# Second weights of the expert layers: high and low halves side by side, two products for three, and a sum of two parts on VectorE

## The reference

```
x = x + 0.5 * _L0_ffn_ref(_layernorm(x), Wg, W1, W2)       # moe0
x = x + _L0_attn_ref(_layernorm(x), ...)
x = x + 0.5 * _L0_ffn_ref(_layernorm(x), Wg, W1, W2)       # moe2
x = x + 0.5 * _L1_ffn_ref(_layernorm(x), Wr, W1, b1, W2, b2)   # moe3
x = x + _L1_attn_ref(_layernorm(x), ...)
x = x + 0.5 * _L1_ffn_ref(_layernorm(x), Wr, W1, b1, W2, b2)   # moe6
```

```
h = gelu(x @ w1 + bb1)
y = h @ w2 + bb2
acc = acc + ce[..., None] * y
```

## Time and profile before

| what | value |
|---|---|
| median of 3 runs | 1114.45 us (1113.37 to 1115.78) |
| profiled execution | 1116.47 us, its span 1114.7 us |
| PE busy | 674.6 us, 5992 matmuls |
| DVE busy | 723.4 us |
| ACT busy | 524.2 us |
| POOL busy | 540.8 us |
| adds and copies of `finish` | from 106.0 to 156.9 (moe0), 388.2 to 439.2 (moe2), 547.5 to 668.8 (moe3), 904.2 to 1062.1 (moe6) |

### The profile page before, as it was taken

One profiled execution on the slowest core, in us unless ns is written; L12 is line 12 of the kernel. 1 busy time (PEld: TensorE's weight loads), 2 busy tenths in 40 slices (PEclk: granted clock), 3 DMA queues, 4 the chain that ended last, 5 costly groups with the idle time before them and its releaser, 6 DMA issues.

```text
span 1114.7 us, 20298 instructions
## 1 busy us (share of the span) xinstructions
PE 674.6 (61%) x5992; PEld 531.0 (48%) x5992; DVE 723.4 (65%) x2283; ACT 524.2 (47%) x1160; POOL 540.8 (49%) x562
## 2 busy tenths in 40 slices
PE   7115853589810586343899981488872569977900
PEld 7013531277710354343688870255552458766700
DVE  7884675989988355677355663599988636533542
ACT  3611333756550133251577871377762258755700
POOL 0007656586100562642676766465112656574475
PEclk9998985789955599555799995699885679988965
DMA  9602321000020133121233331111000123222242
GB/s 300 171 0 48 91 60 48 19 4 2 2 76 0 42 83 70 47 81 28 59 85 77 82 62 50 31 36 36 25 29 29 38 58 83 66 69 63 55 109 71
DMA packets 82502, 66.40 MB, mean 60 GB/s; under 512 B 10665, under 2 KB 74026, under 8 KB 82402
## 3 DMA queue, kind: packets, MB, share of 16 engines
q1 hardware_dynamic: 68674, 37.09, 11.5%
q0 software_dynamic: 13728, 28.02, 11.4%
HBM read 38.99 MB, written 26.08 MB: 58 GB/s over the span
## 4 chain that ended last, share of the span: by engine, by line
PE 24%; DVE 15%; issue 8%; another core or an unknown queue 6%; POOL 6%; ACT 3%; DMA 2%; DVEq 1%; POOLq 0%; ACTq 0%
POOL rt L1284 5%; PE bank L741 4%; PE bank L759 3%; PE bank L743 3%; PE bank L762 3%; PE bank L742 3%; PE bank L760 2%; DVE turned L1114 2%; PE bank L725 1%; DVE x L1172 1%; POOL ytok_loop L1284 1%; DVE arena L2025 1%; DMA rt<-y_moe,slot_i 1%; DVE arena L2018 1%
## 5 line engine op out<-in xcount | busy, mean ns | idle before, releaser
L1261 POOL DMA_INDIRECT turned<-xrows_moe,token x234 | 252.0, 1077 | 326.6 <-DVE token L1034 203.2
L1284 POOL DMA_INDIRECT rt<-y_moe,slot_i x176 | 174.9, 994 | 140.1 <-DVE x L1172 54.6
L817 ACT ACTIVATE turned<-bank,b1T 128x256 f32<-128x256 f32 (+1 forms) x372 | 131.5, 445 | 104.2 <-PE bank L743 47.1
L741 PE MATMUL bank<-rt,w1h 128*128 128x128 bf16 (+1 forms) x528 | 139.2, 264 | 27.9 <-issue 9.7
L759 PE MATMUL bank<-w2h,turned 128*128 x780 | 147.8, 224 | 10.0 <-issue 4.9
L760 PE MATMUL bank<-w2h,turned 128*128 x780 | 147.4, 224 | 9.8 <-issue 9.7
L1114 DVE TENSOR_TENSOR turned<-turned 128x1024 bf16<-128x1024 f32 (+1 forms) x119 | 127.3, 1070 | 34.0 <-ACT turned L822 19.0
L762 PE MATMUL bank<-w2l,turned 128*128 x780 | 133.8, 224 | 11.5 <-issue 10.9
L742 PE MATMUL bank<-rt,w1h 128*128 128x128 bf16 (+1 forms) x528 | 137.3, 261 | 1.7 <-issue 1.6
L743 PE MATMUL bank<-rt,w1l 128*128 128x128 bf16 (+1 forms) x528 | 137.0, 260 | 1.2 <-issue 1.2
L808 ACT ACTIVATE turned<-bank 128x512 f32<-128x512 f32 x40 | 24.0, 599 | 165.9 <-issue 86.4
(11 more groups left out here) (331 smaller groups left out, 1666.3 us busy)
## 6 DMA issues: line engine op xcount, KB each, us to landing
y_moe<-arena SPq DMA_DIRECT2D x119, 128.0 KB
xrows_moe<-xn SPq DMA_DIRECT2D x8, 512.0 KB
turned<-xrows_moe,token POOLq DMA_INDIRECT x234
rt<-y_moe,slot_i POOLq DMA_INDIRECT x176
x<-in_x SPq DMA_DIRECT2D x4, 512.0 KB, 5.9
arena<-in_w SPq DMA_DIRECT2D x1, 2048.0 KB, 9.6
xn<-in_w SPq DMA_DIRECT2D x8, 256.0 KB, 4.8
xrows_moe<-arena SPq DMA_DIRECT2D x4, 512.0 KB
```

Of the source, the lines that this page charges most:

```text
L741: nc.tensor.matmul(o, wh, xh_t, start=True, stop=False)
L817: last = nc.scalar.activation(s["h32"][:, t % 2, o:o + width], bank[1 + 2 * (t % 2) + u // 2][:, at:at + width], ACT.Gelu, bias=b1T[:, ds( ...
L1261: nc.gpsimd.indirect_dma_start(out=s["xs"][:, 2 * (t % BODY) + j], out_offset=None, in_=s["xdram"], in_offset=bass.IndirectOffsetOnAxis(ap ...
L1284: nc.gpsimd.indirect_dma_start(out=brought_to(s, n), out_offset=None, in_=s["ydram"][0:P * UNITS] if s["halves"] == 2 and at < PART else s ...
```

## The change

The high and low halves of the second weights, until now two tiles, become one in which they stand side by side for each chunk (w2_0, w2_1, with an axis of 2 before the last). In `down`, hh times [wh | wl] is one matmul of 256 columns, whose two halves go to different columns of the bank, and hl times wh, of 128 columns, is added to the first half: two matmuls in place of three for each chunk and tile, 780 fewer in all. Each tile of a pair now takes 256 columns of its bank, and the result is the sum of the two halves.

`finish` makes this sum. Without bias, a reduction over the two halves takes the place of the copy. With bias, the add of the bias stays and is followed by a wait for it (semaphore "biased") and a second add, of the bank's second halves to the buffer, in place. A tile's weights have one register operation per chunk where there were two. The instructions that split the weights write the same values to the new places, with a stride.

```diff
-        w2h0, w2l0 = (sb(f"w2{h}0", [P, E, FC0, P], BF16) for h in "hl")
+        w2_0 = sb("w2_0s", [P, E, FC0, 2, P], BF16)
...
-        w2h1, w2l1 = (sb(f"w2{h}1", [P, E, FC1, P], BF16) for h in "hl")
+        w2_1 = sb("w2_1s", [P, E, FC1, 2, P], BF16)
...
-                    nc.scalar.activation(w2h0[:, o], st_w2_0[:, o], ACT.Copy).then_inc(pr["w0h"], 1)
+                    nc.scalar.activation(w2_0[:, o, :, 0], st_w2_0[:, o], ACT.Copy).then_inc(pr["w0h"], 1)
...
-                nc.vector.tensor_tensor(lo[:, o], st[:, o], hi[:, o], ALU.subtract).then_inc(pr["w1l"], 1)
+                h = part(hi, o)
+                nc.vector.tensor_tensor(part(lo, o), like(st[:, o], h), h, ALU.subtract).then_inc(pr["w1l"], 1)
...
+                                       inv=2 * K, idx=halves, half=(K - 1) * NT, turned=n // 2, up=n // 2, gelu=n // 2 * bias, biased=n // 2 * bias, comb=NT,
...
                 k, r, js = t % BODY, t % 2, js_of(t)
-                y = [bank[5 + r][:, P * j:P * j + P] for j in range(2)]
-                w2hf, w2lf = (w[:].rearrange("p e c n -> p (e c n)") for w in (w2h, w2l))
+                both = [bank[5 + r][:, W * j:W * j + W] for j in range(2)]
+                y = [bank[5 + r][:, W * j:W * j + P] for j in range(2)]
+                w2f = w2[:].rearrange("p e c i n -> p (e c i n)").rearrange("p (a i) -> p a i", i=2)
                 pe.wait_ge(*s.at("y", t + 1))
                 pe.wait_ge(*s.at("low", t + 1 + RING))
                 for u in range(FC):
                     hh, hl = ([s[n][:, k % 4, W * u + P * j:W * u + P * j + P] for j in range(2)] for n in ("hh", "hl16"))
-                    for group in (js,) if s["pure"][t] else [(j,) for j in js]:
-                        wh, wl = (w[:, ds(e[group[0]] + P * u, P)] for w in (w2hf, w2lf))
-                        for j in group:
-                            nc.tensor.matmul(y[j], hh[j], wh, start=(u + j == 0), stop=False)
-                            nc.tensor.matmul(y[j], hl[j], wh, start=False, stop=False)
-                        for j in group:
-                            last = nc.tensor.matmul(y[j], hh[j], wl, start=False, stop=(u == FC - 1 and j == js[-1]))
+                    for j in js:
+                        first = e[0] if s["pure"][t] else e[j]
+                        w = w2f[:, ds(first + P * u, P)].rearrange("p a i -> p (a i)")
+                        nc.tensor.matmul(both[j], hh[j], w, start=(u + j == 0), stop=False)
+                        last = nc.tensor.matmul(y[j], hl[j], w[:, 0:P], start=False, stop=(u == FC - 1 and j == js[-1]))
                 last.then_inc(s["down"], 1)
...
                 dve.wait_ge(*s.at("down", t + 1 + RINGS["down"]))
                 dve.wait_ge(ystored[k % YRING], YSTORED[k % YRING][s["index"]] + 16 * turns)
-                y = bank[5 + k % 2][:, 0:W].rearrange("p (j n) -> p j n", j=2)
+                y, ylow = (bank[5 + k % 2][:].rearrange("p (j i n) -> p j i n", j=2, i=2)[:, :, i] for i in range(2))
                 if s["bias"]:
                     unit = 2 * t if A == P else t
                     if unit % BODY == 0:
                         packs.append(dve.value_load(pair_e[0:1, ds(unit // BODY, 1)], min_val=0, max_val=E ** BODY - 1))
                     e = [dve.snap((packs[-1] // E ** (unit % BODY + j)) % E * P) for j in range(1 if s["pure"][t] else 2)]
                     if s["pure"][t]:
-                        last = nc.vector.tensor_tensor(ysb[:, k % YRING], y, b2_all[:, ds(e[0], P)].unsqueeze(1).to_broadcast([P, 2, P]),
-                                                       ALU.add)
+                        nc.vector.tensor_tensor(ysb[:, k % YRING], y, b2_all[:, ds(e[0], P)].unsqueeze(1).to_broadcast([P, 2, P]),
+                                                ALU.add).then_inc(s["biased"], 1)
                     else:
-                        for j in range(tiles_of(s["stage"], t)):
+                        js = tiles_of(s["stage"], t)
+                        for j in range(js):
                             last = nc.vector.tensor_tensor(ysb[:, k % YRING, j], y[:, j], b2_all[:, ds(e[j], P)], ALU.add)
-                    last.then_inc(s["y"], 1)
+                        last.then_inc(s["biased"], 1)
+                    dve.wait_ge(*s.at("biased", t + 1))
+                    js = tiles_of(s["stage"], t)
+                    nc.vector.tensor_tensor(ysb[:, k % YRING, 0:js], ysb[:, k % YRING, 0:js], ylow[:, 0:js], ALU.add)\
+                        .then_inc(s["y"], 1)
                 else:
-                    nc.vector.tensor_copy(ysb[:, k % YRING], y).then_inc(s["y"], 1)
+                    js = tiles_of(s["stage"], t)
+                    nc.vector.tensor_reduce(ysb[:, k % YRING, 0:js], bank[5 + k % 2][:, 0:W * js].rearrange("p (j i n) -> p j n i", i=2, n=P),
+                                            AX, ALU.add).then_inc(s["y"], 1)
```

More of the change, by code:

```diff
@@ L149, in program @@
         spare = [w[:].rearrange("p a b -> p (a b)") for w in (w1h0, w1l0)] + \
-                [w[:].rearrange("p a b c -> p (a b c)") for w in (w2h0, w2l0)]
+                [w2_0[:, a:b].rearrange("p a b i c -> p (a b i c)") for a, b in ((0, E // 2), (E // 2, E))]
         x2n = spare[0].bitcast(F32).rearrange("p (k n f) -> p k n f", k=2, n=B)
@@ L243, in program @@
         splits = []
-        for st, hi, lo, loads in ((st_w1_1, w1h1, w1l1, ("w1", 16)), (st_w2_1, w2h1, w2l1, ("w1b", 16 * E))):
-            spec = "p a b -> p (a b)" if st is st_w1_1 else "p a b c -> p (a b c)"
-            splits.append((st, hi[:].rearrange(spec), lo[:].rearrange(spec), loads))
+        for st, hi, lo, loads in ((st_w1_1, w1h1, w1l1, ("w1", 16)), (st_w2_1, w2_1[:, :, :, 0], w2_1[:, :, :, 1], ("w1b", 16 * E))):
+            if st is st_w1_1:
+                part = lambda a, o: a.rearrange("p e f -> p (e f)")[:, o]
+            else:
+                part = lambda a, o: a.rearrange("p e c n -> p (e c) n")[:, o.start // P:o.stop // P]
+            splits.append((st, hi, lo, part, loads))
         PIECES = E * F1 // SPLIT
@@ L258, in cast, with like @@
                     o = slice(E // 2 * (i - 6), E // 2 * (i - 5))
-                    nc.scalar.activation(w2h0[:, o], st_w2_0[:, o], ACT.Copy).then_inc(pr["w0h"], 1)
+                    nc.scalar.activation(w2_0[:, o, :, 0], st_w2_0[:, o], ACT.Copy).then_inc(pr["w0h"], 1)
             return cast
+        def like(a, b):
+            return a if len(b.shape) == len(a.shape) else a.rearrange("p (c n) -> p c n", n=P)
         def split_high(act):
-            for st, hi, lo, (q, v) in splits:
+            for st, hi, lo, part, (q, v) in splits:
                 act.wait_ge(ld[q], v)
@@ L267, in split_high @@
                     o = slice(SPLIT * i, SPLIT * (i + 1))
-                    nc.scalar.activation(hi[:, o], st[:, o], ACT.Copy).then_inc(pr["w1h"], 1)
+                    h = part(hi, o)
+                    nc.scalar.activation(h, like(st[:, o], h), ACT.Copy).then_inc(pr["w1h"], 1)
         def split_low(dve, which):
-            st, hi, lo, loads = splits[which]
+            st, hi, lo, part, loads = splits[which]
             for i in range(PIECES):
@@ L426, in norm0_vector @@
             dve.wait_ge(pr["w0h"], 4)
-            nc.vector.tensor_tensor(w2l0[:], st_w2_0, w2h0[:], ALU.subtract).then_inc(pr["w0l"], 1)
+            nc.vector.tensor_tensor(w2_0[:, :, :, 1].rearrange("p e c n -> p (e c) n"), st_w2_0.rearrange("p e c n -> p (e c) n"),
+                                    w2_0[:, :, :, 0].rearrange("p e c n -> p (e c) n"), ALU.subtract).then_inc(pr["w0l"], 1)
         def ln_halves(dve, s, blocks):
@@ L622, in moe @@
                                        xhi=(2 - K) * (n // 2), onehot=2 * K,
-                                       inv=2 * K, idx=halves, half=(K - 1) * NT, turned=n // 2, up=n // 2, gelu=n // 2 * bias, comb=NT,
+                                       inv=2 * K, idx=halves, half=(K - 1) * NT, turned=n // 2, up=n // 2, gelu=n // 2 * bias, biased=n // 2 * bias, comb=NT,
                                        **{q: RINGS[q] + n // 2 for q in RINGS}))
@@ L690, in moe_tensor @@
                 last.then_inc(s["inv"], 1)
-            (w1h, w1l), (w2h, w2l) = s["w1"], s["w2"]
+            (w1h, w1l), w2 = s["w1"], s["w2"]
             pairs = s["pairs"]
@@ L2152, in gau_vector @@
                 scales_and_heads(five, six, j + 1)
-        W0 = dict(FC=FC0, w1=(w1h0, w1l0), w2=(w2h0, w2l0), wr=wrc[:, 0, :], bias=False, top2=False)
-        W1 = dict(FC=FC1, w1=(w1h1, w1l1), w2=(w2h1, w2l1), wr=wrc[:, 1, :], bias=True, top2=True)
+        W0 = dict(FC=FC0, w1=(w1h0, w1l0), w2=w2_0, wr=wrc[:, 0, :], bias=False, top2=False)
+        W1 = dict(FC=FC1, w1=(w1h1, w1l1), w2=w2_1, wr=wrc[:, 1, :], bias=True, top2=True)
         in_order = list(range(NT))
```

## The result

The changed kernel takes 1096.47 us in the median of 4 runs (1094.34 to 1098.21), the kernel before, run beside it, 1113.91 (1113.15 to 1115.78).

A forecast was written before the change was run, and what follows sets the result against it. PE's instruction queue was taken to bound mixed pairs, gathers with late news of PE's work the pure ones. Terms -6.9-2.6+0.5+0.49+0.6-0.3 = -8.2 took the median 1114.45 to 1106.2 us; range 1097 to 1120.

The forecast's parts named there:

- Mixed pairs, -6.9: moe6's mixed pairs: down product falls from 1.86 to 1.40 us, 14 two-tile pairs and 2 single; -6.9 us, bounds 0 to -8.0.
- five rows of equal cost: Mixed down products: 232 ns for five queue rows a triple, so three cost about 139 ns and columns' 166 become the limit.
- Pure pairs, 0: Pure pairs' down product: columns unchanged and the array is the limit, so 0; bounds 0 to the hole of 0.35 us.
- the hole is timed by the gathers alone: moe3's pure pairs: PE's 0.35 us idle gap in the down product ends by the gather's time, not by PE's.
- fewer queued instructions close the hole: Rival, moe3's pure pairs: 16 matmuls instead of 24 outlast PE's 0.35 us gap; -12 us, to 1094; chance 0.17.
- moe0 and moe2, -2.1: moe0 and moe2 loops: PE saves 2.6 us behind the last gathers, DVE's reduction costs 0.5 at the last pairs.
- The bias pairs' second add, +0.49 at the end of moe3 and nothing in the loops: DVE's extra add in 79 bias pairs: hidden in the loops, but moe3's last add delays the store, +0.49 us.
- first rival: Pure pairs: DVE's second add lies in the loop, 0.23 us in each of 63 pairs, 14.5 us slower, 1120.7; chance 0.20.
- The end of moe6, +0.6: End of moe6: the last two pairs' second adds stand ahead of the closing fetches; +0.6 us, bounds 0.5 and 1.0.
- third rival: moe6's mixed pairs: their gain is lost to the next wait, leaving about 1113.5 us; chance 0.13.
- second rival: moe3's pure pairs: fewer queued instructions close PE's 0.35 us gap; 1094 us, or 1100 at half; chance 0.17.

The follow-up runs named there:

- e6: Kernel before with joined weight layout, one register operation a triple instead of two, still three matmuls (low-weight product replaced by a repeat): 1011.68 us, ratio 0.9981 to before, short condition.
- e11: The change with each 256-column down matmul cut into two of 128, all else kept: 1130.27 us, ratio 1.0075 to the kernel before, long condition.
- e1: The change with each 256-column down matmul cut into two of 128, all else kept: 1018.77 us, ratio 1.0042 to the kernel before, short condition.
- e2: Kernel before with only the joined layout of the second weights; old matmuls, register operations, copies and adds: 1017.96 us, ratio 1.0032, short condition.
- e7: The change with a third DVE wait and add in each of the 79 bias pairs: 1008.68 us, ratio 0.9965 to the kernel before, short condition.
- e8: Kernel before, separate weight tiles, with a second DVE wait and operation (a maximum) in the 79 bias pairs: ratio 1.0013 to before, short condition.
- e15: Kernel before, separate weight tiles, with a second DVE wait and maximum in the 79 bias pairs, compared again: ratio 1.0029 to before, short condition.

## Why the prediction was right or wrong, point by point

*Sign and mechanism*: the sign is right, and so is the mechanism that was priced: PE's instruction queue is the limit in products that name their weights anew for each tile, and VectorE's second part is almost free. But what was priced, mixed pairs with moe0 and moe2, gave some 9 of the 16 us by the traces; the pure pairs, put at nothing, gave 6.4.

*Mixed pairs, -6.9*: right in kind; the product gains more than the term, and the loop less. 1.86 us before came from one pair, the middle of the stretches is 1.90 and 1.93, and the 1.40 after held a margin for the first operation that is not there: 1.33. That is 0.58 x 14 = 8.1 in the products of two tiles. The two single ones, put at half of a pair, take 0.68 and 0.87 us for their own matmuls before and 0.66 and 0.67 after. But the stretches of mixed pairs got only 5.9 us shorter. In the first half the stretch gains what its products gain (4.3 us, against 0.58 x 7 = 4.1), in the second only 1.6 of some 4, since there PE now waits for DVE's low parts ahead of the down product, for 2.9, 4.4 and 2.1 us in the three traces of the change where it was 0.7 in each trace of before. PE's waits between the first and the last down product of these eight pairs, before and in the change (us in total, times, longest):

```profile
PE bank L759 <- DVE turned L1114: 0.7, 2, 0.5
```

```profile
PE bank L770 <- DVE turned L1123: 2.9, 1, 2.9
```

The reason that stood beside the term, five rows of equal cost, was wrong: e6 shows that one register operation is worth all of it, as four rows go as fast as three.

*Pure pairs, 0*: this is the step that failed, by the most us. The runs show 6.4 us in its place, 2.3 in moe3 and 4.1 in moe6. The term rested on two claims, that the array is the limit and that the hole is timed by the gathers alone. The first holds where there is no hole (2.87 to 2.85), except for the three pairs of each half of moe6 with a mixed up product behind: 0.5 each in the short condition. In the long one the three intervals of the first half, from down product to down product, are 0.7 shorter together (1.5 in the short one); those of the second half are too uneven to tell. I had looked at the down product between its own two ends and not at the lead that it gives to what comes next. The second claim doesn't hold: with fewer instructions the middle pair of moe3 falls from 3.15 and 3.29 to 2.85, and with the wide matmul cut in two it is 3.15 again. This was the rival "fewer queued instructions close the hole", priced at 12 us in moe3; it took place at a fifth of that price, since larger holes take the place of the small ones. The 4.1 us in moe6 go the same way: in e11 its pure pairs take 98.2 us again, as before, in one trace. Why a shorter queue meets fewer holes is not shown.

*moe0 and moe2, -2.1*: -3.1 in the loops of the long condition. The reduction's duration was right. That it counts only behind the last pair is borne out in the short condition, where the two loops of e1 are 0.7 us longer than e2's, together; in the long one it wasn't tested by itself, and e11's are 3.3 longer than before's.

*The bias pairs' second add, +0.49 at the end of moe3 and nothing in the loops*: right. +0.45 there. e7, e8 and e15 in the short condition and the pure pairs of e11 in the long one are far below the first rival's 14.5 us.

*The end of moe6, +0.6*: measured -1.0 in the long condition, with a spread of 1.1 between traces of the change. In the short condition it is +6: POOL's fetches become the bound there, which no rival of mine had at the end of the kernel. The third rival (the mixed pairs' gain lost to the next wait) is true to half there, and in the long condition it is true of the last eight pairs, by DVE's low parts.

*The number*: 1094 to 1100 was the time of the second rival, and 1096.5 was measured, but by another sum: 5.9 of mixed pairs, 3.1 of moe0 and moe2, 6.4 of pure pairs, 1.0 at the end, less 0.3 between the loops. So it is luck that the time is the rival's. The range began at 1097 and took in half of that rival; the bounds of -8.0 for mixed pairs and of -10.8 for moe0 and moe2 together would have carried it lower.

## What to carry to other kernels

Where a matmul's address is computed at run time, count the register operations between matmuls ahead of the matmuls: in one layout, one of them less for every three matmuls took a product of 24 short matmuls from 2.05 to 1.35 us. Pairing halves of weights in one tile is a way to share an address, while two addresses inside one tile cost more than in two tiles (2.05 against 1.92). Judge the saving of instructions by the queue's lead as well, in what comes behind. And ask what waits next when a loop gets shorter: here half of the mixed pairs' gain could end in the fetches behind the loop, or in the low parts ahead of the last products.

## What the runs showed of the hardware that I had not expected

The same kernel took 1014 or 1114 to 1122 us at different times, one chip showing both. The traces differ in how late the other engines hear of PE's work: the middle of the time from the last down matmul's start to DVE's add is 0.47 us in moe3 in the short condition and 2.3 to 2.6 in the long one for the kernel before, and what lies between moe3's and moe6's loops is longer too (208 to 212 against 234 to 236 us). In moe3 the granted clock is 0.99 to 1.00 in both (the earlier trace rows and the stretches above), so it is not PE's clock that makes the difference there. What sets the condition is not known and wasn't tested; the trace of e2 has 90 us of moe3 in which PE never stops, and no trace of the long condition has that.
